# Pair 1's query projection by seven half products, and value tiles ahead of query tiles

## The reference

```
x = x + _L0_xattn_ref(_layernorm(x), ctx_4096, ctx_4096, mask, Wq, Wk, Wv, Wo)
...
NUM_Q_HEADS, NUM_KV_HEADS, KEY_SIZE = (32, 8, 128)
q = (query @ Wq).reshape(b, t, h, d)      # here 1024 rows x 512, 32 heads of 128
k = (key @ Wk).reshape(b, t, kv_h, d)
v = (value @ Wv).reshape(b, t, kv_h, d)
q = apply_rope(q)
k = apply_rope(k)
logits = jnp.einsum('btkgd,bTkd->bkgtT', q, k) * ATTN_MULT
logits = MAX_ATTN_VAL * jnp.tanh(logits / MAX_ATTN_VAL)
weights = jax.nn.softmax(jnp.where(mask, logits, -1e+30), axis=-1)
attn = jnp.einsum('bkgtT,bTkd->btkgd', weights, v).reshape(b, t, h * d)
return attn @ Wo
```

## Time and profile before

| | us |
|---|---|
| median of 3 timed executions | 823.64 (823.53 to 824.62) |
| the profiled execution | 825.46 |
| its span, first to last instruction | 823.7 |
| PE busy | 815.2 |
| DVE busy | 591.5 |
| POOL busy | 430.0 |
| ACT busy | 403.7 |

### The profile page before, as it was taken

The page is one execution under the profiler, slowest core; times in us unless marked ns, Lnnn a source line. Parts: engine busy times, 40 slices in busy tenths (PEclk is TensorE's granted clock), DMA queues, the critical chain, the costliest instruction groups (busy, mean ns, idle before and its releaser), DMA issues.

```text
span 823.7 us, 12087 instructions
## 1 busy us (share of the span) xinstructions
PE 815.2 (99%) x4310; PEld 674.5 (82%) x4310; DVE 591.5 (72%) x1133; ACT 403.7 (49%) x980; POOL 430.0 (52%) x341
## 2 busy tenths in 40 slices
PE   9999999899999999999999999999999999999998
PEld 7898877677777778777778788898988888888887
DVE  6874449889797988879788656464365667677894
ACT  6542114332334332343431532667797877777762
POOL 4665449874769667677864620113232531366442
PEclk9999999899999999999999999999999999999999
DMA  8545310413233223322311840002011200300002
GB/s 313 228 152 170 91 61 4 128 53 104 77 103 102 78 65 88 118 64 77 103 53 54 296 119 14 26 27 52 14 39 26 65 27 14 128 14 2 0 1 103
DMA packets 33244, 67.00 MB, mean 81 GB/s; under 512 B 5152, under 2 KB 8480, under 8 KB 32544
## 3 DMA queue, kind: packets, MB, share of 16 engines
q1 hardware_dynamic: 30640, 61.38, 24.0%
q10 hardware_dynamic: 2544, 4.85, 1.6%
HBM read 54.55 MB, written 11.67 MB: 80 GB/s over the span
## 4 chain that ended last, share of the span: by engine, by line
PE 73%; POOL 1%; issue 1%; DVE 0%; ACT 0%; DMA 0%; ACTq 0%; POOLq 0%
PE PB L1814 14%; PE PB L1816 13%; PE PB L1815 13%; PE PB L1862 11%; PE PB L2077 8%; PE PB L2092 3%; PE PB L1821 3%; PE PB L2004 3%; PE PB L1987 2%; PE PB L2025 1%; PE PB L2039 0%; POOL W L1200 0%; DMA stage<-in_wo 0%; POOL WVl L1200 0%; POOL WSl L1200 0%
## 5 line engine op out<-in xcount | busy, mean ns | idle before, releaser
L1237 POOL TENSOR_TENSOR qb<-qb,arena 128x512 f32<-128x512 f32 x76 | 99.6, 1316 | 126.2 <-DVE arena L1656 126.2
L1314 ACT ACTIVATE Oh<-PB 96x128 fp32r<-96x128 f32 (+2 forms) x236 | 79.3, 359 | 45.7 <-PE PB L2004 26.6
L1528 DVE TENSOR_TENSOR xs<-xs,PB 128x512 f32<-128x512 f32 x111 | 73.2, 682 | 36.8 <-PE PB L1816 27.9
L1200 POOL TENSOR_TENSOR WVl<-stage,WVh 128x512 fp32r<-128x512 f32 (+1 forms) x25 | 31.6, 1278 | 70.6 <-ACT WVh L1314 64.0
L1653 DVE TENSOR_TENSOR qb<-PB,ropeq 128x512 f32<-128x512 f32 x64 | 44.0, 688 | 26.6 <-PE PB L1816 16.1
L1814 PE MATMUL PB<-WVh,Oh 128*128 128x512 f32 x158 | 62.3, 394 | 0.8 <-DVE arena L1656 0.4
L1815 PE MATMUL PB<-WVl,Oh 128*128 128x512 f32 x158 | 61.5, 390 | 0.0
L1816 PE MATMUL PB<-WVh,Ol 128*128 128x512 f32 x158 | 61.5, 389 | 0.0
L1314 ACT ACTIVATE WSh<-wsum 128x1024 fp32r<-128x1024 f32 x12 | 12.7, 1061 | 90.8 <-POOL wsum L1182 90.8
L1814 PE MATMUL PB<-W,Oh 128*128 128x512 f32 x142 | 55.5, 391 | 0.6 <-POOL W L1200 0.6
L1815 PE MATMUL PB<-W,Oh 128*128 128x512 f32 x142 | 55.3, 389 | 0.0
(11 more groups left out here) (336 smaller groups left out, 2464.4 us busy)
## 6 DMA issues: line engine op xcount, KB each, us to landing
stage<-in_wq SPq DMA_DIRECT2D x44, 256.0 KB, 2.8
stage<-in_wo SPq DMA_DIRECT2D x44, 256.0 KB, 2.8
arena<-recs SPq DMA_DIRECT2D x32, 256.0 KB, 3.9
stage<-in_wk SPq DMA_DIRECT2D x12, 256.0 KB, 4.4
keys<-qb SPq DMA_DIRECT2D x12, 256.0 KB, 2.3
arena<-keys SPq DMA_DIRECT2D x6, 512.0 KB, 3.3
xs<-in_x SPq DMA_DIRECT2D x8, 256.0 KB, 6.6
ctx_hi<-cTh SPq DMA_DIRECT2D x1, 2048.0 KB, 7.4
```

Of the source, the lines that this page charges most:

```text
L1200: e.tensor_tensor(lo, src, hi.bitcast(f32), ALU.subtract).then_inc(s_wlo)
L1237: e.tensor_tensor(dst, dst, tmp, ALU.add).then_inc(s_radd)
L1314: return e.activation(dst, src, ACT.Copy)
L1528: e.tensor_tensor(xs[:, i, :], xs[:, i, :], PB[b][:, :], ALU.add).then_inc(free[b])
```

## The change

`PLAIN` goes from 2 to 1, so that pair 1 is made by seven half products too, and only pair 0 stays plain. Pair 1's weight sums and pair step stand among the `vq` tiles. All `vq` tiles come ahead of the first `q0` tile. `b0(0)` comes before q0(1,3) and q0(1,2) instead of behind pp(0,0); the four `xt_split` steps are spread out; `sum0(0)` moves ahead of pp(0,1); `b0(1)` comes ahead of pp(0,2); and `norm0(0)` stands behind the first cmb of pair 1.

```diff
--- before.py
+++ after.py
@@ -8,7 +8,7 @@
 NU = 16
 N1 = 32
 LO, HI = range(0, 4), range(4, 8)
-PLAIN = 2
+PLAIN = 1
 D0_BANKS = (0, 1, 4, 6)
 SLOTS = (4, 5, 6, 7, 0, 1, 2, 3)
 PARTS = {1: (0, 256), 2: (256, 512), 4: (512, 768), 5: (768, 1024), 6: (1024, 1280), 7: (1280, 1536), 3: (1536, 1792)}
@@ -305,25 +305,24 @@
     pair(0)
     k0(7, 1)
     spill_k(7, 0)
-    for n in range(4):
-        vq(n + 2)
-        if n == 0:
-            spill_k(7, 1)
-            split("wq0", 2)
-        else:
-            spill_v(n + 1)
+    vq(2)
+    spill_k(7, 1)
+    split("wq0", 2)
+    for n in range(3, 8):
+        vq(n)
+        spill_v(n - 1)
+        if n == 4:
+            step("sums", 1)
+            pair(1)
+    spill_v(7)
+    q0(0, 0)
+    step("xt_split", 0, 0)
+    for n in range(1, 4):
         q0(0, n)
-        if n == 3:
-            q0(1, 1)
-    vq(6)
-    spill_v(5)
-    q0(1, 0)
-    q0(1, 3)
-    vq(7)
-    spill_v(6)
-    spill_v(7)
-    pair(1)
     ring.remove(2)
+    for n in (1, 0):
+        q0(1, n)
+    step("xt_split", 0, 1)
 
     def products(u, *ks):
         for k in ks:
@@ -350,30 +349,34 @@
                     e0_add(u - 2, c)
 
         if u == 0:
-            step("sums", 2)
+            burst(0)
+            q0(1, 3)
+            q0(1, 2)
             q0p(0, 0, 5)
-            burst(0)
-            q0p(0, 1, 7)
-            q0(1, 2, bank=1)
-            for k in range(2):
-                for h in range(2):
-                    step("xt_split", k, h)
-            q0p(0, 2, 0)
-            q0p(0, 3, 4)
             step("sum0", 0)
             step("sum0_out", 0)
+            step("xt_split", 1, 0)
+            q0p(0, 1, 7)
             continue
         if u == 1:
+            burst(1)
+            step("xt_split", 1, 1)
+            q0p(0, 2, 6)
+            q0p(0, 3, 4)
             for n in range(2):
                 split("wp", 2, n)
-            q0p(1, 0, 6)
-            burst(1)
+            products(1, 1, 2)
+            norm0(0)
+            products(1, 5)
+            rope_p(1, 0)
             step("k_in", 2)
-            q0p(1, 1, 1)
-            q0p(1, 2, 0)
+            products(1, 6, 3)
+            rope_p(1, 1)
+            products(1, 7)
+            rope_p(1, 2)
             step("pair", 2)
-            norm0(0)
-            q0p(1, 3, 4)
+            products(1, 4)
+            rope_p(1, 3)
             for n in range(4):
                 split("wo0", n)
             continue
```

## The result

| | before | after |
|---|---|---|
| median, us (8 executions each, same chip) | 824.59 (823.53 to 826.07) | 827.77 (825.23 to 828.46) |
| profiled execution, us | 825.46 | 827.57 |
| its span, us | 823.7 | 825.7 |

The ratio is 1.0038, 95% interval 1.0026 to 1.0049: 3.2 us slower, and beyond the bound of 0.2%. The forecast was 828.0, range 823.9 to 830.3.

What follows compares the result with a forecast made beforehand. PE was taken as the bound (busy 815.2 of 823.7 us). Removed -1.36 -2.71 -3.25, idle +5.0 +2.4, half clock +1.36 +2.72 +0.5 gave +4.7, taken as +4.4 on 823.64: 828.0 us, range 823.9 to 830.3.

Steps and rivals of the forecast that it cites:

- The two waits: PE waits 5.0 us at pair 1's product 4 for cmb(1,7), then 2.4 at pair 2's first product for rope (1,3).
- The sum of 23.2 us: VectorE's queued steps from 126.4 us to the end of cmb(1,7), at 149.6; PE has only 18.4 us of work.
- The rule on the shared port: VectorE and GpSimd lock a port pair; xt_split(1,1) and norm0(0) could be 0.5 and 0.8 us shorter, but rows were followed.
- The clock: Half clock from about 147 to 160 us, adding 1.36 for product 4, 2.72 for pair 2's products 1 and 2, 0.5 after.
- The base: The forecast's starting time: 823.64 us, median of three timed runs of the kernel before; its profiled span was 823.7.
- The sum in the trace: Net delay at the end of pair 2's d0 and b0: +4.7 us, from 159.81 to 164.5.
- the 3.25 us of half clock: In the kernel before, d0 and b0 of pair 2 took 7.05 instead of 3.80 us; counted as removed.
- Behind it: After d0 and b0, stages are unchanged and packed, so the rest passes to the end; +4.4 us taken.
- Clock kept: Rival: both waits come but full clock holds through them; +0.6, 824.2 us, chance 0.11.
- The wait just goes: Rival: VectorE isn't late at product 4, nothing stands; -7.3, 816.3 us; chance 0.09 for gone or mostly gone.
- More behind: Rival: half clock lasts through b0, or POOL's adds become the later one; +6 to +8.3, 830 to 832 us, chance 0.07.

Runs made afterwards that it cites:

- the bank's run: Changed kernel with pair 1's products 1, 6, 7 and 4 in bank 1 instead of bank 5: 824.67 us, +0.3 against before.
- the run with xt_split forward: Changed kernel with xt_split(0,1), (1,0) and (1,1) moved forward among the query tiles: 826.26 us, +1.9 against before.
- the one with norm0 moved: Changed kernel with norm0(0) moved on VectorE from behind pair 1's first cmb to behind its third: 827.51 us, +3.1 against before.
- The spare matmuls: Changed kernel with 15 unused matmuls ahead of pair 1's product 4 and 10 ahead of pair 2's first product: 825.71 us, +1.3 against before.
- the spare matmuls in the kernel before: Kernel before the change, with 10 unused matmuls of 512 columns put ahead of d0(0): 823.98 us, -0.4 against before.
- with VectorE relieved: New order with pair 1 by plain tiles, xt_split steps forward, pair 2's weight sums behind sum0(0): 820.27 us, -4.1 against before.
- the run with the third cmb first: Changed kernel with bank 1, xt_split and pair 2's sums forward, plus pair 1's third cmb ahead of rope (1,1): 822.28 us, -2.1 against before.

## Why the prediction was right, and where it was off

**The two waits.** Right in place and cause: the bank's run takes the second away alone, and the run with xt_split forward shortens the first by what VectorE has less to do. The first was forecast at 5.0 us and recorded as 3.70 (4.09 - 0.23 = 3.86 between slots, 144.83 to 148.92), the second at 2.4 and recorded as 2.63 (2.83 between slots). Without the start's 0.45 us VectorE ended the third cmb at 148.3, forecast 149.6. The sum of 23.2 us, from 126.4, was mis-sized: sum0(0) took 4.03 instead of 4.55, xt_split(1,1) 1.14 instead of 1.73; norm0 took 2.27 instead of 2.07, and the ropes 0.4 less in all. For sum0(0) and xt_split(1,1) I had taken what such an instruction took where GpSimd was busy for what it costs.

**The rule on the shared port.** The Trainium skill (SBUF — State Buffer, "Who interferes with whom") was right where I let the row decide: xt_split(1,1) came first, at 135.10, and took 1.23 us, 0.5 less, as the forecast's use of the rule gave. The one that stood was GpSimd's addition, which started at 135.15 and took 2.34 us, where the one before it took 1.28. On norm0 the rule was right and my use of it wrong: GpSimd was not idle, norm0 started at 141.09 inside the adds of two ropes (139.79 to 142.35) and took 2.34. The additions into rec above are the plainest sign of an exclusive lock: held to the mask's end where they came second, not held where they came first.

**The clock.** Right that it falls, and the stage. Of the new kernel's terms this one was mis-sized most: 4.6 us were forecast for product 4, products 1 and 2 and d0 (1.36 + 2.72 + 0.5). It was about 0.6 for product 4 (it fell only amid it), 1.5 for products 1 and 2 (153.75 to 158.01 = 4.26 against 2.72), and none for d0. The step that failed was to count the clock's return from the moment at which PE goes on, 6.4 us of work as in the earlier trace rows. By the slices (0.87 in the one from 149 is 0.74 us at full and 0.26 at half clock) half clock was granted for 6.8 us in both traces, from 152.3 to 159.2 before and from 149.7 to 156.6 after; forecast was about 147 to 160. In the changed kernel the wait of 2.8 us lay inside, where a low clock costs nothing, so only 2.7 us of work ran slow behind it. Nor is 6.8 us a rule: it was 3.4 us in the trace with xt_split forward and 10.2 in the one with norm0 moved. The spare matmuls price the clock at 1.9 us in the median.

**The base.** The sum in the trace was +4.7, less 0.3 behind it; the trace shows +2.0 in the span (+1.6 without the start), and the medians +3.2. That the forecast of 828.0 was met within 0.3 us is luck, since errors cancel. The waits and the clock of the new kernel were over-sized by about 3 us (11.98 forecast, 8.8 measured). Against that, the 3.25 us of half clock that I took off from before is in the profiled execution, but of 85 others 42 had a mean clock of 1.0, and the spare matmuls in the kernel before gave 0.4 us: the median gains much less from its going. And the median of three that I added to was 0.95 us under the median of eight.

**Behind it.** "The rest passes to the end" was right for this change: the wait at pair 3 stayed at 0.5 us, and the span grew by what d0(0)'s stage had lost. It isn't so the other way: kernels that came to d0(0) earlier gave part of it back behind it. With spare matmuls in the kernel before, 3.2 us were gained at pair 2's product 5 and 1.2 were left at the end of the trace.

**The rivals.** "Clock kept" did not come, as the clock fell. What it would have been is shown by the spare matmuls: +1.3 against before, where +0.6 was forecast. "The wait just goes" did not come either; what the order was worth without the half products is -1.8, and -4.1 with VectorE relieved. "More behind" did not come: the clock was full before d0(0), and VectorE stood only 0.70 us for GpSimd at the rope (1,2). That the shared bank was a cause of its own, and the cheaper one to undo (-2.9 us by one number), I had in the sum but not among the rivals.

## What to carry to other kernels

Work saved on the bounding engine counts only if the engine that serves it has the time: 6 matmuls (1.36 us) were bought with three VectorE additions (2.1 us) at a place where VectorE was already behind. Sum the serving engine's queue from the moment at which it stops waiting up to the instruction that is waited for, and compare with the bounding engine's work over the same stretch; and look at who shares the bank with a result that comes late. After a gain, look one stage on for what gives it back before you believe it. And time the base as often as the change, since one profiled execution may be of the rare kind.

## What was not expected of the hardware

The kernel before, with its hole of 2.5 to 2.7 us ahead of d0(0) in the trace, did not lose the clock every time: 42 of 85 executions had a mean clock of 1.0, 39 had 0.998, and 4 lost as much as the profiled one (0.996). With holes of 0.9 and 1.2 us the mean was 1.0 in all 6 executions. A 64x32 addition on VectorE (0.25 us) took up to 2.39 us and ended 0.04 to 0.05 us after GpSimd's 128x1024 mask in the three traces shown, so a small instruction can stand as long as the other engine's largest. It depends on which of the two comes first: started 0.45 us ahead of the mask, it took 0.53 us.

Open are why the median of the kernel with spare matmuls gained more than its trace, where the rest of the gain went in the run with the third cmb first, and what seven products would do for pair 1 in the old order.
